# Short chained clears on GpSimd between the row scatters of a cross-attention and mixture-of-experts kernel

## The chip, the cores and the metric

The kernel runs on one core of one Trainium2 chip. The metric is the device time of one execution in microseconds (us). Three runs of the kernel before stand beside it; their median is 516.37 us. Engines are named as in the profile: PE is TensorE (matmuls) and PEld its weight loads, DVE is VectorE, ACT is ScalarE, POOL is GpSimd, SP is SyncE, which here only issues transfers.

## The reference

One layer over 4096 tokens (64 sequences of 64) of width 256: attention over a context and the tokens themselves, then a mixture of 32 experts, 4 for each token, beside a shared expert.

```python
h = layernorm(x)
q, k_new, v_new = h @ wq.T, h @ wk.T, h @ wv.T
k, v = concat([ctx, k_new]), concat([ctx, v_new])            # 64 + 64 keys of each sequence
x = x + softmax(q @ k.T / 16) @ v @ wo.T
h = layernorm(x)                                             # rows of 256
probs = softmax(h @ router.T)                                # 32 experts
topv, topi = top_k(probs, 4); topv = topv / sum(topv)
out = sum over the 4 experts e of topv[e] * (silu(h @ w_gate[e]) * (h @ w_up[e])) @ w_down[e]
out = out + sigmoid(h @ sgate_w) * ((silu(h @ sw_gate) * (h @ sw_up)) @ sw_down)
x = x + out
```

## The kernel before, in words

**Attention.** The tokens are worked in 16 blocks (`blocks`) of 256 tokens. Every engine runs its own software-pipelined loop over a step number n (L604 on ACT, L888 on PE, L1293 on DVE); what step n does for the different stages belongs to the blocks n+2 down to n-5. On PE a step has four groups of three-term products (L806: queries, keys, values, context values, 12 matmuls of 256 columns each), transposes, the scores (L981), the attended values (L998) and the router's logits (L1012).

**Routing and the scatter.** DVE normalizes the attended rows of block b into `rows[:, b % RING]` (`normalize`, L1222, in step b+3), a ring of RING = 6 buffers. It finds the 4 experts of each row, and the row's place with each, and as the last piece writes the weights into the ring (`weights`, L1289, in step b+5). GpSimd then scatters the block: 2 tiles of 128 rows times 4 experts are 8 indirect transfers (`send`, L481), each of 128 rows of 268 words, to the table `sent` in HBM. Before each transfer `send` waits for the block's numbers, names, weights and places; these come with L1289, so only a block's first transfer really waits. Before DVE writes block b+6 into the ring it waits for `rows_sent` of block b (L1317). After the last table entry is made, SP waits once for all scatters (L403 to L405) and then loads the experts' tiles (L417, L419), which PE turns (L1049).

**GpSimd's order** is written out in two loops (L496 to L502). For each step n there are 8 turns; turns 0 to 3 send what is left up to block n-6, turns 4 to 7 up to block n-5. So a step sends the second half of one block and then the first half of the next one. GpSimd takes nothing from the step number itself: it runs through this order and stops only at the semaphores in `send`. From step 17 on (n > blocks) each transfer is followed by one short clear (`breathe`, L490) of `pause`, four small tiles that nobody reads; the last 12 transfers are followed by three each. A clear there waits only for the one four places before it.

```python
for n in range(-2, blocks + 4):
    for turn in range(SENT_A_STEP):
        if may_send(n - 6 if turn < 4 else n - 5):
            send()
            if n > blocks:
                breathe(1)
```

**After attention**, PE works the shared expert for token groups 1 to 3, then 68 pairs of expert tiles, then the shared expert for groups 4 to 7, which end the kernel; GpSimd scatters the experts' results (L512).

Of the kernel before, what the change touches and what calls it, by code (L numbers as in the profile page):

```python
# [35 lines left out]
def build_xattn_moe(nc, x, ctx_t, wq_t, wk_t, wv, wo_t, router_t, w_gate_up, w_down,  # L36
# [34 lines left out]
    with ExitStack() as stack:  # L71
        def sb(name, shape, dt=F32):
            return stack.enter_context(nc.sbuf_tensor(name, shape, dt))
# [99 lines left out]
        pause = [sb(f"pause{n}", [P, 24]) for n in range(4)]  # L173
# [89 lines left out]
        def wait(eng, name, count):  # L263
            if count > 0:
                eng.wait_ge(S[name], count)
# [82 lines left out]
        def _(sp):  # L348
# [57 lines left out]
            for pair in range(pairs):  # L406
                u = pair % RING
                first, size = column_of(pair), QUARTER if mixed(pair) else P
                _, at = nc.values_load_multi_w_load_instructions(
                    tile_row[0:1, first:first + (5 if mixed(pair) else 2)], engines=[mybir.EngineType.SP],  # L410
                    min_val=0, max_val=EXPERTS * tokens - size,
                    skip_runtime_bounds_check_because="a tile's first row is a row of an expert's "
                                                      "region, at most its count less a tile on")
                wait(sp, "turned_psum", pair - RING + 1)
                wait(sp, "back_ready", (pair - RING) // 2 + 1)
                for q in range(P // size):
                    sp.dma_start(loaded[size * q:size * q + size, u, 0, :].bitcast(F32), sent[bass.ds(at[q], size), :]) \  # L417
                        .then_inc(tile_in[u], 16)
                sp.dma_start(loaded[:, u, 1, :].bitcast(F32), sent[bass.ds(at[P // size], P), :]).then_inc(tile_in[u], 16)  # L419
# [14 lines left out]
        @block.gpsimd  # L434
        def _(pool):
            c = S["consts"]
            pool.memset(ident[:, :], 0.0).then_inc(c, 1)
            pool.memset(before[:, :], 1.0).then_inc(c, 1)
            pool.memset(upto[:, :], 1.0).then_inc(c, 1)
            pool.memset(no_row, 0.0).then_inc(c, 1)  # L440
            pool.wait_ge(c, 4)
            pool.affine_select(out=ident[:, :], in_=ident[:, :], compare_op=ALU.not_equal, fill=1.0,
                               base=0, pattern=[[-1, P]], channel_multiplier=1).then_inc(c, 1)
            pool.affine_select(out=before[:, :], in_=before[:, :], compare_op=ALU.is_ge, fill=0.0,
                               base=-1, pattern=[[1, P]], channel_multiplier=-1).then_inc(c, 1)
            pool.affine_select(out=upto[:, :], in_=upto[:, :], compare_op=ALU.is_ge, fill=0.0,
                               base=0, pattern=[[1, EXPERTS]], channel_multiplier=-1).then_inc(c, 1)
            pool.iota(iota_e[:, :], [[1, EXPERTS]], base=0, channel_multiplier=0,
                      allow_small_or_imprecise_dtypes=True).then_inc(c, 1)
            pool.iota(place_no[:, :, :], [[P * TOP, tiles], [1, TOP]], base=P * slot_tiles, channel_multiplier=TOP,  # L450
                      allow_small_or_imprecise_dtypes=True).then_inc(c, 1)
            pool.iota(taken[0][:, 0, :], [[tokens // P, EXPERTS]], base=0, channel_multiplier=0,
                      allow_small_or_imprecise_dtypes=True).then_inc(c, 1)
            pool.memset(ones_h[:, :], 1.0).then_inc(c, 1)
            pool.iota(slot_no[:, :], [[P, slot_tiles]], base=0, channel_multiplier=1,
                      allow_small_or_imprecise_dtypes=True).then_inc(c, 1)
            pool.iota(region[:, :], [[0, 1]], base=0, channel_multiplier=tokens,
                      allow_small_or_imprecise_dtypes=True).then_inc(c, 1)
            pool.iota(lane[:, :], [[0, 1]], base=0, channel_multiplier=1,
                      allow_small_or_imprecise_dtypes=True).then_inc(c, 1)  # L460
            pool.iota(lanes_after[:, :], [[0, 1]], base=P - 1, channel_multiplier=-1,
                      allow_small_or_imprecise_dtypes=True).then_inc(c, 1)
            pool.memset(ones_e[:, :], 1.0).then_inc(c, 1)

            pool.wait_ge(c, POOL_CONSTS)

            sends = [(b, j, k) for b in range(blocks) for j in range(2) for k in range(TOP)]
            sent_now = [0]
            breaths = [0]

            def send():
                b, j, k = sends[sent_now[0]]
                sent_now[0] += 1
                u = b % RING
                if b == 0:
                    pool.wait_ge(S["no_rows"], 16 * HEADS)
                wait(pool, "numbered", b + 1)
                wait(pool, "named_ready", b + 1)
                wait(pool, "weights_ready", b + 1)
                wait(pool, "slot_ready", b + 1)  # L480
                pool.indirect_dma_start(  # L481
                    out=sent,
                    out_offset=bass.IndirectOffsetOnAxis(ap=slot[:, 2 * b + j, k:k + 1], axis=0),
                    in_=rows[:, u, j, :], in_offset=None).then_inc(rows_sent[u], 16)

            def breathe(times):

                for _ in range(times):
                    wait(pool, "breath", breaths[0] - len(pause) + 1)
                    pool.memset(pause[breaths[0] % len(pause)][:, :], 0.0).then_inc(S["breath"], 1)  # L490
                    breaths[0] += 1

            def may_send(n):
                return sent_now[0] < len(sends) and sends[sent_now[0]][0] <= n

# [3 lines that stand above are left out]
                        send()  # L499
                        if n > blocks:  # L500
                            breathe(1)
            while sent_now[0] < len(sends):  # L502
                send()
                breathe(3)

            for pair in range(pairs):
                u = pair % DOWNS
                wait(pool, "back_ready", pair // 2 + 1)
                wait(pool, "down_ready", pair + 1)
                for s in range(2):  # L510
                    t = 2 * pair + s
                    pool.indirect_dma_start(  # L512
                        out=returned,
                        out_offset=bass.IndirectOffsetOnAxis(ap=back[:, t:t + 1], axis=0),
                        in_=down_e[u][:, s, :], in_offset=None).then_inc(down_sent[u], 16)

        @block.scalar
        def _(act):
# [174 lines left out]
            def experts_to_copy(pair):  # L693

                first = column_of(pair)
                more = 7 if mixed(pair + 2) else 0
                _, values = nc.values_load_multi_w_load_instructions(
                    tile_expert[0:1, first:first + 4 + more], engines=[mybir.EngineType.Activation],
                    min_val=0, max_val=EXPERTS - 1,
                    skip_runtime_bounds_check_because="a tile's first row over the rows of a region "  # L700
                                                      "is the number of an expert")
                copied_e[pair], copied_e[pair + 2] = values[0:4], values[7:11]
# [85 lines left out]
        def _(pe):  # L788
# [288 lines left out]
            def experts_of(pair):  # L1077
                first = column_of(pair) + (4 if mixed(pair) else 0)
                _, values = nc.values_load_multi_w_load_instructions(
                    tile_expert[0:1, first:first + (1 if mixed(pair) else 2)], engines=[mybir.EngineType.PE],  # L1080
                    min_val=0, max_val=EXPERTS - 1,
                    skip_runtime_bounds_check_because="a tile's first row over the rows of a region "
                                                      "is the number of an expert")
                return values
# [678 lines left out]
```

## Time and profile before

| | |
|---|---|
| median of 3 runs | 516.37 us (515.13 to 516.96) |
| span of the profiled execution | 667.5 us |
| busy share of the span | PE 86%, PEld 72%, DVE 54%, ACT 43%, POOL 40% |
| mean granted TensorE clock | 0.903 of full speed |

For the profiled execution the page gives its span alone, no time around it. It is 151 us longer than the median of the runs, so its durations are those of a slower execution, and only its order and its ratios are taken over without care. The attention loop is the part from some 20 us to 250 us of the span, the rest of routing and the shared expert's first groups follow until 340 us, the experts' tiles until 593 us, and the last shared groups until the end.

### The profile page before, as it was taken

The numbers are of one execution on the slowest core, as the hardware profiler recorded it, in microseconds if no ns is written. First come the engines' busy times: TensorE is split into PE (matmuls) and PEld (weight loads), VectorE is DVE, ScalarE is ACT, GpSimd is POOL, SyncE is SP. The second block draws the span as 40 slices with busy tenths as digits, with TensorE's granted clock in tenths as the row PEclk, the third lists the DMA queues.
The fourth block names the chain that finished last, engine by engine and source line by source line (L and its number), as shares of the span: only waits on it lengthen the run. The fifth ranks groups of instructions, "written<-read, shape, count | busy, mean of one in ns | idle before, by whom it ended". The sixth has DMA issues, their size and how long they took to land. (4 is left out here: it accounts for less than half of the span.)

```text
span 667.5 us, 13365 instructions
## 1 busy us (share of the span) xinstructions
PE 574.4 (86%) x3945; PEld 478.3 (72%) x3945; DVE 363.5 (54%) x1199; ACT 288.7 (43%) x719; POOL 269.4 (40%) x344
## 2 busy tenths in 40 slices
PE   8998787788887777899998988778877898979998
PEld 7997777677777565677886666656666676658886
DVE  5575455555555351565553635445454444536998
ACT  5775444555444440613463545444454544401111
POOL 1004444445555458380034544445454454560000
PEclk9999788987778788699997977988989978989999
DMA  5573544444433322293145444544444544228996
GB/s 160 181 227 128 170 156 129 144 134 145 138 123 113 110 76 107 70 244 98 31 130 148 131 140 124 140 136 139 130 140 140 150 131 132 87 86 330 368 340 230
DMA packets 65956, 100.77 MB, mean 151 GB/s; under 512 B 9856, under 2 KB 52864, under 8 KB 65792
## 3 DMA queue, kind: packets, MB, share of 16 engines
q1 hardware_dynamic: 48704, 60.30, 30.6%
q0 software_dynamic: 12672, 35.41, 14.7%
q10 hardware_dynamic: 4512, 4.23, 1.9%
q8 instruction: 34, 0.56, 0.4%
q14 instruction: 34, 0.28, 0.1%
HBM read 55.92 MB, written 43.97 MB: 150 GB/s over the span
## 5 line engine op out<-in xcount | busy, mean ns | idle before, releaser
L512 POOL DMA_INDIRECT returned<-arena,back x136 | 130.6, 960 | 171.7 <-DVE back L1629 81.5
L481 POOL DMA_INDIRECT sent<-rows,slot x128 | 129.9, 1015 | 159.2 <-issue 82.7
L1100 PE MATMUL bank<-w_gu,arena 128*128 x416 | 94.7, 363 | 26.6 <-issue 16.6
L1100 PEld LDWEIGHTS bank<-w_gu,arena 128*128 128x128 f32 x416 | 73.0, 205 | 32.8 <-issue 32.8
L1580 DVE TENSOR_TENSOR arena<-bank,arena 128x192 f32<-128x192 f32 x68 | 24.2, 356 | 113.5 <-ACT arena L737 94.5
L737 ACT ACTIVATE arena<-bank 128x192 f32<-128x192 f32 x68 | 22.3, 329 | 127.0 <-remote 70.5
L806 PE MATMUL bank<-w_hi_all,att_split 128*128 128x256 f32 x256 | 56.8, 314 | 18.6 <-issue 18.6
L1597 DVE TENSOR_SCALAR arena<-bank,back_to 128x256 f32<-128x256 f32 x136 | 59.0, 476 | 6.3 <-remote 5.3
L806 PE MATMUL bank<-att_split,w_hi_all 128*128 128x256 f32 x256 | 55.5, 336 | 1.4 <-issue 1.3
L710 ACT COPY hnt<-w_gu 128x384 f32 x128 | 55.7, 509 | 0.0
L806 PEld LDWEIGHTS bank<-w_hi_all,att_split 128*128 128x128 f32 x256 | 42.4, 208 | 18.2 <-issue 18.2
L806 PE MATMUL bank<-hnt_rounded,ws_hi 128*128 128x512 f32 x160 | 51.0, 412 | 2.6 <-issue 2.6
L806 PEld LDWEIGHTS bank<-att_split,w_hi_all 128*128 128x128 f32 x256 | 47.7, 248 | 4.7 <-issue 4.6
L539 ACT ACTIVATE act_t<-bank 128x512 f32<-128x512 f32 x24 | 14.2, 598 | 82.9 <-PE bank L806 66.6
L1049 PE MATMUL bank<-ident_r,loaded 128*128 128x128 f32 x272 | 46.0, 295 | 0.4 <-issue 0.4
L850 PE MATMUL bank<-ws_d,act_t 128*128 128x256 f32 x192 | 43.3, 381 | 1.0 <-DVE act_t L1241 1.0
L731 ACT COPY arena<-bank 128x512 f32<-128x512 f32 x68 | 39.5, 582 | 8.9 <-PE bank L1049 2.5
L850 PEld LDWEIGHTS bank<-ws_d,act_t 128*128 128x128 f32 x192 | 36.1, 190 | 6.4 <-DVE act_t L1241 1.4
L806 PEld LDWEIGHTS bank<-hnt_rounded,ws_hi 128*128 128x128 f32 x160 | 31.6, 197 | 10.9 <-issue 4.0
L1049 PEld LDWEIGHTS bank<-ident_r,loaded 128*128 128x128 f32 x272 | 32.6, 148 | 9.0 <-issue 2.8
L806 PE MATMUL bank<-w_lo_all,att_split 128*128 128x256 f32 x128 | 30.3, 310 | 6.8 <-issue 6.5
L1311 DVE TENSOR_REDUCE negmax<-bank 128x2 f32<-128x256 f32 x16 | 6.7, 422 | 51.8 <-remote 51.8
(216 smaller groups left out, 1128.6 us busy)
## 6 DMA issues: line engine op xcount, KB each, us to landing
arena<-returned SPq DMA_DIRECT2D x16, 1024.0 KB, 7.2
loaded<-sent SPq DMA_DIRECT2D x104, 134.0 KB
w_gu<-w_gate_up SPq DMA_DIRECT2D x32, 192.0 KB
sent<-rows SPq DMA_DIRECT2D x4, 1072.0 KB, 6.2
loaded<-sent SPq DMA_DIRECT2D x128, 33.5 KB
resid<-x SPq DMA_DIRECT2D x16, 256.0 KB, 2.9
att_plain<-ctx_t SPq DMA_DIRECT2D x16, 256.0 KB, 3.1
out<-resid ACTq DMA_DIRECT2D x7, 512.0 KB, 4.9
```

The source lines that it names most:

```text
L481: pool.indirect_dma_start(out=sent, out_offset=bass.IndirectOffsetOnAxis(ap=slot[:, 2 * b + j, k:k + 1], axis=0), in_=rows[:, u, j, :], in ...
L512: pool.indirect_dma_start(out=returned, out_offset=bass.IndirectOffsetOnAxis(ap=back[:, t:t + 1], axis=0), in_=down_e[u][:, s, :], in_offs ...
L539: act.activation(act_t[:, f, :], gate_banks[f % 2][:, :], ACT.Silu) \
L710: last = act.copy(gu_copy[:, q, :, :], w_gu[:, :, bass.ds(copied_e[pair][q], 1), :] .rearrange("p c e f -> p c (e f)"))
L731: act.copy(gt[pair % 2].rearrange("p s c q -> p (s c q)"), gt_banks[pair % 2][:, :]) \
L737: act.activation(act_e[pair % 2], gu_views[pair % 2][:, :, 0:F], ACT.Silu) \
L806: last = pe.matmul(out_view, stationary(s_part, c), moving(m_part, c), start=(n == 0 and c == 0), stop=(n == 2 and c == DC - 1))
L850: last = pe.matmul(sum_banks[t // 2][:, 256 * (t % 2):256 * (t % 2) + 256], act_t[:, f, P * t:P * t + P], ws_d[:, f, :], start=(f == 0 and ...
L1049: last = pe.transpose(gt_banks[pair % 2][:, at:at + P].bitcast(F32R), loaded[:, u, s, P * c:P * c + P], ident_r[:, :])
L1100: last = pe.matmul(view[:, s, :], rows_t[:, s, c, :], w_gu[:, c, bass.ds(e[s - 2 + len(e)], 1), :] .rearrange("p e f -> p (e f)"), start=( ...
L1580: dve.tensor_tensor(act_e[pair % 2], gu_views[pair % 2][:, :, F:2 * F], act_e[pair % 2], ALU.mult).then_inc(S["act_e_ready"], 1)
L1597: last = dve.tensor_scalar(down_e[u][:, s, :], down_banks[pair % 2][:, D * s:D * s + D], back_to[:, pair // 2 % 4, 2 * (pair % 2) + s, 0:1 ...
```

## The change

Within attention (steps up to n = 16), behind turn 2, turn 5 and turn 7 of each step that sends, GpSimd makes four short clears of `pause`. Each of them waits for the one just before it. The semaphore `breath` has no other reader than GpSimd.

```diff
+            def rest(times):
+
+                for _ in range(times):
+                    wait(pool, "breath", breaths[0])
+                    pool.memset(pause[breaths[0] % len(pause)][:, :], 0.0).then_inc(S["breath"], 1)
+                    breaths[0] += 1
+
             def may_send(n):
                 return sent_now[0] < len(sends) and sends[sent_now[0]][0] <= n
 
@@ -499,6 +506,8 @@
                         send()
                         if n > blocks:
                             breathe(1)
+                        elif turn in (2, 5, 7):
+                            rest(4)
```

## Rows read from the trace of the kernel before

**Rows 1.** The page, parts 1 and 2: engines, slices, and the clock granted to PE.

```profile
PE 574.4 (86%) x3945; PEld 478.3 (72%) x3945; DVE 363.5 (54%) x1199; ACT 288.7 (43%) x719; POOL 269.4 (40%) x344
...
PEclk9999788987778788699997977988989978989999
```

**Rows 2.** Waits from 56 to 236 us: engine and line, waited for, us, times, longest.

```profile
POOL sent L481 <- DVE rows L1289: 60.8, 11, 6.2
DVE negmax L1311 <- remote: 51.8, 11, 9.6
ACT logits L616 <- remote: 50.2, 11, 6.6
```

**Rows 3.** Timeline of POOL over one block's eight transfers and the next's first.

```profile
118.94 0.96 POOL L481 DMA_INDIRECT sent<-rows,slot  x1 [5.77 <-DVE rows L1289]
120.20 1.12 POOL L481 DMA_INDIRECT sent<-rows,slot  x1 [0.30 <-issue]
121.63 1.35 POOL L481 DMA_INDIRECT sent<-rows,slot  x1 [0.30 <-issue]
123.28 0.96 POOL L481 DMA_INDIRECT sent<-rows,slot  x1 [0.30 <-issue]
...
128.33 0.96 POOL L481 DMA_INDIRECT sent<-rows,slot  x1 [0.30 <-issue]
134.49 0.95 POOL L481 DMA_INDIRECT sent<-rows,slot  x1 [5.21 <-DVE rows L1289]
```

**Rows 4.** Timeline of POOL: clears unchained and a chain of waits at the start.

```profile
1.15 0.31 POOL L440 MEMSET rows<- 128x268 f32 x1
1.70 0.29 POOL L442 TENSOR_SCALAR_AFFINE_SELECT ident<-ident 128x128 f32<-128x128 f32 x1 [0.24 <-POOL rows L440]
...
249.30 0.97 POOL L481 DMA_INDIRECT sent<-rows,slot  x1 [0.17 <-issue]
250.27 0.14 POOL L490 MEMSET pause<- 128x24 f32 x1
250.57 0.97 POOL L481 DMA_INDIRECT sent<-rows,slot  x1 [0.16 <-issue]
...
282.43 0.23 POOL L490 MEMSET pause<- 128x24 f32 x3
```

**Rows 5.** Line L1222 on DVE, 56 to 236 us: ns min/median/max.

```profile
L1222 DVE TENSOR_SCALAR rows<-resid,both_moments,rstd x24: 403/406/429, 65.4 to 235.7; 128x256 f32<-128x256 f32 x24
L1222 DVE TENSOR_SCALAR att_plain<-resid,both_moments,rstd x20: 396/404/415, 55.8 to 198.1; 128x256 f32<-128x256 f32 x20
```

**Rows 6.** The same line in the drain, 249 to 251 us.

```profile
L1222 DVE TENSOR_SCALAR rows<-resid,both_moments,rstd x2: 404/469/534, 249.5 to 249.8; 128x256 f32<-128x256 f32 x2
```

**Rows 7.** Timeline of DVE in the step of rows 3.

```profile
118.65 0.72 DVE L1222 TENSOR_SCALAR att_plain<-resid,both_moments,rstd 128x256 f32<-128x256 f32 x2
...
122.06 0.69 DVE L1296 TENSOR_TENSOR att_split<-att_plain,att_split 128x512 fp32r<-128x512 f32 x1
124.03 0.69 DVE L1300 TENSOR_TENSOR att_split<-bank,att_split 128x512 fp32r<-128x512 f32 x1 [1.28 <-issue]
127.88 0.42 DVE L1311 TENSOR_REDUCE negmax<-bank 128x2 f32<-128x256 f32 x1 [3.16 <-remote]
128.22 0.75 DVE L1222 TENSOR_SCALAR rows<-resid,both_moments,rstd 128x256 f32<-128x256 f32 x2
```

**Rows 8.** Timeline of POOL: first and last transfer of block 1.

```profile
71.70 0.96 POOL L481 DMA_INDIRECT sent<-rows,slot  x1 [5.28 <-DVE rows L1289]
...
81.13 0.96 POOL L481 DMA_INDIRECT sent<-rows,slot  x1 [0.30 <-issue]
```

**Rows 9.** SP's wait for all scatters, its first tile load, and PE's first use.

```profile
SPq L405 <- DMA sent<-rows,slot: 21.8, 1, 21.8
...
303.79 0.38 SPq L417 DMA_DIRECT2D loaded<-sent  x1
...
L1049 PE MATMUL bank<-ident_r,loaded x272: 223/249/668, 324.3 to 576.1; 128*128 128x128 f32 x136
```

**Rows 10.** Timeline of PE: four products at either level of its clock.

```profile
119.10 0.64 PE L806 MATMUL bank<-w_hi_all,att_split 128*128 128x256 f32 x4
...
131.92 1.05 PE L806 MATMUL bank<-att_split,w_hi_all 128*128 128x256 f32 x4
```

**Rows 11.** Stretches between blocks' first transfers: POOL busy, granted clock, DMA share, GB/s.

```profile
118.94:134.49 15.55, 8.21 (x9) 0.89 0.48 148
134.49:150.09 15.60, 8.24 (x8) 0.80 0.42 135
150.09:166.23 16.14, 8.24 (x9) 0.77 0.45 141
```

## The prediction

> **What bounds the kernel now.** I began with the engines' busy shares and the clock row of the page [rows 1]: PE is busy for 86% of the span and POOL for 40%. PE is the engine to watch, and its granted clock falls below full speed in most slices of attention. Then the waits inside attention, from 56 to 236 us [rows 2]. POOL waits 60.8 us in 11 places for the weights of L1289, about 5.5 us in each step; DVE waits 51.8 us in 11 places before its row maximum L1311 and ACT 50.2 us before the logits copy, both behind PE's work. No wait of PE, ACT or DVE in that view is put down to POOL or to a transfer. The step is thus paced by PE with DVE and ACT behind it, and POOL is the engine with room. The stretches between the first transfers of successive blocks show the pace: 15.55, 15.60 and 16.14 us a step, of which POOL is busy 8.2 [rows 11].
>
> The reader should then look at one block's transfers [rows 3]. Eight transfers run from 118.94 to 129.29 us, 0.96 us each and 0.30 us apart, and POOL is idle for 5.21 us before the next block's first at 134.49. The second and third take 1.12 and 1.35 us, the ones that lie beside DVE's burst of SBUF work.
>
> **The change, part by part.** How many clears. Sending begins with step 5, whose turns 4 to 7 send, so two rests fall there; steps 6 to 16 have three each. That is 2 + 33 = 35 rests of four clears, 140 in all. Counted in a block's own order, a rest comes behind its second, fourth and seventh transfer, since a step's turns 4 to 7 are a block's first half. Nothing is removed and no instruction of another engine is touched. The first clear of attention's rests and the breaths later on use the same semaphore, and later breaths find their counts long reached.
>
> One rest. A clear takes 0.14 us [rows 4]. Clears that don't chain follow each other closely: three take 0.23 us together. A chained one has to see its predecessor's semaphore; the nearest row is the first of the constants, which starts 0.24 us after the clear it waits for has ended (1.46 to 1.70 us, rows 4). So a chained clear costs 0.38 us, a rest 0.14 + 3 x 0.38 = 1.28 us. The next transfer then starts 0.17 us behind the last clear instead of 0.30 us behind the last transfer, so a rest holds the queue up by 1.28 + 0.17 - 0.30 = 1.15 us. From below, were the chain free (three in 0.23 us, four in about 0.31), a rest would add 0.18 us. I take 1.15 us, because the row with a real wait is nearer to what is added.
>
> One block. Three rests are 3.5 us. The eight transfers then last from 118.94 to about 132.7 us, and less if the third transfer, moved from 121.63 to about 122.8, no longer lies beside DVE's burst and gives back its 0.39 us. The next block's weights come in time for a start at 134.49 us. About 2 us of the idle 5.21 us are left, and they hide the whole of the change on POOL. Cost on the path: 0.
>
> Who waits for the later transfers. First, DVE before it refills a ring buffer. At 128.22 us it writes block 7 (rows 7, second L1222), which needs block 1's transfers; the last of these started at 81.13 us [rows 8]. That is 46 us of room against 3.5 us of delay. Second, SP before the experts' tiles. Its wait for the scatters lasts 21.8 us and its first load goes out at 303.79 us, but PE first turns a tile at 324.3 us [rows 9], 20 us later. Besides, that wait is for the last blocks, whose transfers are outside the part that gets rests, and POOL stands idle ahead of them. Cost: 0 for both.
>
> Side effects on DVE. Twenty-four and twenty L1222 instructions in attention take 403 to 429 and 396 to 415 ns, whether a transfer runs beside them or not [rows 5]. So transfers don't slow DVE. A clear can: the one L1222 pair in the drain that has a clear beside it (250.27 us, rows 4) has one instruction of 534 ns [rows 6], 128 ns over the usual 406 and about a clear's own length. The Trainium skill says in "SBUF — State Buffer", section "Who interferes with whom", that a VectorE instruction in a two-port mode and a GpSimd instruction exclude each other and that the later one waits in full; by this rule, the trace agrees for the clear with its 128 ns, while rows 5 show nothing of the sort for the transfers. Where do the clears fall? With the times above, at 121.3 to 122.6, 125.0 to 126.3 and 129.9 to 131.2 us of the step shown. DVE's L1222 pairs lie at 118.65 to 119.37 and 128.22 to 128.97 us, outside all three, and the second and third rest lie mostly in its idle time [rows 7]. I count 0 collisions, with 4 a step as the upper bound.
>
> Sum: 0 + 0 + 0. The profiled execution would stay at a span of 667.5 us. The page gives no time around the span, and the median of the runs, 516.37 us, is 151 us below it; since my sum is zero it carries over unscaled, and the forecast is 516.4 us. The measurement can tell about 0.3%, or 1.55 us, from nothing.
>
> **Rivals.**
>
> 1. DVE is held up by the clears (slower). This is the one cost the trace has shown. Place: the four L1222 of each of 12 steps. Price: 48 x 0.128 = 6.1 us if every one met a clear and all lay on the path, giving 522.5 us. It decides from 12 collisions on the path (12 x 0.128 = 1.54 us). For it: the timed runs are faster than the profiled one, so DVE's instructions stand closer around the rests there; the third rest is only 0.9 us behind a pair. Against it: DVE waits 4.7 us a step before L1311, which swallows 0.128 us easily. A likely size is one or two hits a step, 1.5 to 3 us: 518 to 519.5 us. Chance 0.11.
>
> 2. POOL becomes the pace in the timed runs. Scaled by 516.4/667.5, a step of 15.6 us is 12.1 us, while POOL's block, if it does not scale, takes 13.8 us and 0.9 us for the release: 2.6 us too much. Over 11 blocks the transfers fall 28 us behind. The ring's room scales to 36 us, so DVE still doesn't stop; the idle 5 and 10 us ahead of the last blocks take up 12 us of it, and the last 16 us meet the 20 us (scaled 16) between SP's first load and PE's first turn. The result lies at the edge of a cost: 516.4 up to some 520 us. Against it, POOL's own gaps probably shrink too. Chance of over 1.55 us: 0.07.
>
> 3. PE gains its clock or another engine gains from thinner traffic (faster). Four products take 0.64 us at the full 2.4 GHz and 1.05 us at 1.2 GHz [rows 10], 0.10 us each; a step has 48 of them, so one whole step at the higher level is worth 4.9 us: 511.5 us. Neighbouring steps already differ, 0.89, 0.80 and 0.77 of full speed, with the same work [rows 11], so small shifts in what PE waits for can move it, and the transfers would be spread over 13.8 instead of 10.3 us of a step in which the transfer engines are busy for 0.42 to 0.48. Against it: I find no row by which a later transfer makes DVE, ACT or PE earlier, and step lengths don't follow the granted clock (15.60 at 0.80, 16.14 at 0.77, 15.55 at 0.89). The same path could lose time as well, but nothing leads into it. Half a step to a step is 2 to 5 us: 511.5 to 514.5 us. Chance 0.30, rather high for want of a row, since the profiled execution is so unlike the timed ones that a cause could hide between them.
>
> That the change does nothing at all (clears that end inside the 0.30 us gap) would look like my forecast.
>
> **How the numbers follow.** No effect on the path has 0.52 and gives 516.4 us, with a range of its own of 514.9 to 517.9 us. Faster by over 0.3% has 0.30, slower has 0.11 + 0.07 = 0.18. The range for 8 in 10 takes in the same case, rival 3 down to a full step regained and rivals 1 and 2 up to about half of rival 1's bound: 511.5 to 519.5 us, leaving out some 0.08 on either side.
>
> **What the changed profile would show.** 140 more clears at a new line on POOL, four to a group, some 0.38 us apart; the idle time before each block's first transfer down from 5.2 to about 2 us with the waiter and releaser unchanged; the last transfer still ending near 299 us; L1222 at 396 to 429 ns; waits of DVE at L1311 unchanged; steps of 15.5 to 16.1 us. I am wrong if that idle time is gone, if many L1222 take over 0.5 us, or if the steps' lengths or the clock granted in them change together by more than the spread among the three shown.

## The result: slower by 7.7%, and the profile after

The changed kernel takes 553.88 us (median of 4 runs, 553.51 to 555.38) beside 515.75 us for the kernel before, a ratio of 1.077 (95% interval 1.071 to 1.083). Here and below a ratio is the record's own estimate with its interval, not the quotient of the two medians printed beside it; the two differ by up to 1.4%. The forecast was no change, 516.4 us, in a range of 511.5 to 519.5. It is 38 us off, on the side to which it gave 0.18.

One thing has to be said first, as nothing else can be read without it. The chips on which these runs were made fall into two groups. On one, the kernel before takes 512 to 519 us; on the other, 641 to 681 us. Of the four chips of the experiments, numbers 2, 4 and 8 are slow in this sense and number 15 is fast. The times that came with the kernel are of the first group, and the profile on which the prediction rests (span 667.5 us) shows the pace of the second. The profile after (span 553.0 us) is again of the first.

The page of the changed kernel, parts 1 and 2:

```profile
PE 511.7 (93%) x3945; PEld 433.7 (78%) x3945; DVE 363.1 (66%) x1199; ACT 287.0 (52%) x719; POOL 286.6 (52%) x484
...
PE   7999999999978799991399999999999999999998
...
PEclk9999999999979999997599999999999999999999
```

Against [rows 1] PE's clock is hardly ever held back, and PE is busy for 93% of a shorter span. What stands out is a hole in PE's row in slices 19 and 20; the timelines below put it at 251 to 270.5 us. The waits of the same kernel over its whole span (engine and line, waited for, us in total, times, longest), the second list those of SP:

```profile
POOL sent L481 <- issue: 96.6, 118, 52.3
...
DVE rows L1231 <- DMA sent<-rows,slot: 25.4, 5, 6.1
PE bank L1058 <- DMA loaded<-sent: 23.8, 11, 19.6
...
POOL sent L481 <- DVE rows L1298: 2.7, 4, 1.0
```

```profile
SPq L405 <- DMA sent<-rows,slot: 57.8, 1, 57.8
```

The line for POOL's wait for the weights has shrunk from 60.8 us in 11 places [rows 2] to 2.7 us in 4: GpSimd hardly ever runs dry, it has a backlog. Two kinds of waits are new against the old profile, DVE's for the ring (L1231, L1222 of the kernel before) and PE's for a loaded tile (L1058, L1049 of before), the longest 19.6 us. SP's wait for all scatters is 57.8 us long instead of 21.8 [rows 9]. The timelines of DVE and of POOL show the two paces:

```profile
108.42 0.41 DVE L1320 TENSOR_REDUCE negmax<-bank 128x2 f32<-128x256 f32 x1
...
118.03 0.41 DVE L1320 TENSOR_REDUCE negmax<-bank 128x2 f32<-128x256 f32 x1
```

```profile
101.75 0.96 POOL L481 DMA_INDIRECT sent<-rows,slot  x1 [0.30 <-issue]
102.71 0.66 POOL L497 MEMSET pause<- 128x24 f32 x4
104.36 0.97 POOL L481 DMA_INDIRECT sent<-rows,slot  x1 [1.00 <-issue]
...
107.97 0.66 POOL L497 MEMSET pause<- 128x24 f32 x4
109.33 0.98 POOL L481 DMA_INDIRECT sent<-rows,slot  x1 [0.70 <-issue]
```

An attention step takes 9.61 us, not 15.6. GpSimd needs 13.4 to 14.4 us for a block, 13.9 in the mean (the first block's first transfer starts at 56.0 us, the twelfth's at 208.9). It falls some 4 us behind in every step. The end of that queue is what PE finally waits for; SP's, POOL's and PE's timelines at that place:

```profile
263.91 0.97 POOL L481 DMA_INDIRECT sent<-rows,slot  x1 [0.16 <-issue]
```

```profile
267.47 0.38 SPq L417 DMA_DIRECT2D loaded<-sent  x1
```

```profile
245.56 5.34 PE L859 MATMUL bank<-ws_d,act_t 128*128 128x256 f32 x24
270.50 0.72 PE L1058 MATMUL bank<-ident_r,loaded 128*128 128x128 f32 x4 [19.60 <-DMA loaded<-sent]
```

### The profile page after: what moved, and what is told of

It reads as the page before. It is cut to its first block and busy times, and to the rows that moved or that the text cites. A ratio compares the mean times of both kernels' runs of the same rounds, so it can differ in the third digit from the quotient of the medians.

```text
span 553.0 us, 13505 instructions
## 1 busy us (share of the span) xinstructions
PE 511.7 (93%) x3945; PEld 433.7 (78%) x3945; DVE 363.1 (66%) x1199; ACT 287.0 (52%) x719; POOL 286.6 (52%) x484
## 5 line engine op out<-in xcount | busy, mean ns | idle before, releaser
L481 POOL DMA_INDIRECT sent<-rows,slot x128 | 128.7, 1005 | 102.3 <-issue 96.6
L1109 PE MATMUL bank<-w_gu,arena 128*128 x416 | 83.8, 339 | 0.0
L1109 PEld LDWEIGHTS bank<-w_gu,arena 128*128 128x128 f32 x416 | 66.4, 191 | 0.3
L1058 PE MATMUL bank<-ident_r,loaded 128*128 128x128 f32 x272 | 41.9, 278 | 24.2 <-DMA loaded<-sent 23.8
L1058 PEld LDWEIGHTS bank<-ident_r,loaded 128*128 128x128 f32 x272 | 30.0, 142 | 36.3 <-issue 20.3
L548 ACT ACTIVATE act_t<-bank 128x512 f32<-128x512 f32 x24 | 14.4, 599 | 75.9 <-PE bank L815 75.9
L815 PE MATMUL bank<-w_hi_all,att_split 128*128 128x256 f32 x256 | 49.0, 294 | 0.0
L815 PE MATMUL bank<-att_split,w_hi_all 128*128 128x256 f32 x256 | 44.0, 284 | 0.0
L815 PEld LDWEIGHTS bank<-w_hi_all,att_split 128*128 128x128 f32 x256 | 37.4, 192 | 0.9 <-issue 0.9
L815 PEld LDWEIGHTS bank<-att_split,w_hi_all 128*128 128x128 f32 x256 | 36.7, 193 | 0.1
L1278 DVE SCALAR_TENSOR_TENSOR resid<-bank,shared_gate,resid 128x256 f32<-128x256 f32 x28 | 11.7, 478 | 30.8 <-PE bank L859 30.4
L1231 DVE TENSOR_SCALAR rows<-resid,both_moments,rstd 128x256 f32<-128x256 f32 x32 | 12.1, 418 | 25.4 <-DMA sent<-rows,slot 25.4
```

The lines of the kernel that those rows point to most:

```text
L481: pool.indirect_dma_start(out=sent, out_offset=bass.IndirectOffsetOnAxis(ap=slot[:, 2 * b + j, k:k + 1], axis=0), in_=rows[:, u, j, :], in ...
L548: act.activation(act_t[:, f, :], gate_banks[f % 2][:, :], ACT.Silu) \
L815: last = pe.matmul(out_view, stationary(s_part, c), moving(m_part, c), start=(n == 0 and c == 0), stop=(n == 2 and c == DC - 1))
L1058: last = pe.transpose(gt_banks[pair % 2][:, at:at + P].bitcast(F32R), loaded[:, u, s, P * c:P * c + P], ident_r[:, :])
L1109: last = pe.matmul(view[:, s, :], rows_t[:, s, c, :], w_gu[:, c, bass.ds(e[s - 2 + len(e)], 1), :] .rearrange("p e f -> p (e f)"), start=( ...
```

## The experiments

Theories, as the expectations name them. **A**: where PE is at full rate, GpSimd's queue sets when the experts' tiles can be loaded, and a rest costs what it delays the queue. **B**: the clears hold DVE up. **C**: the clears cost by themselves. **D**: at the slower pace, rests keep PE at full rate. **E**: the pace of PE is a matter of the chip alone.

### The kernel before once more (e0_before)

No edit.

> The kernel before once more, for a profile at the pace of the timed runs; the profile on which the prediction rested was 151 us longer than they are. Theory A (GpSimd is the pace): an attention step is about 9.6 us, as in the profile of the changed kernel, a block's eight transfers take 8 x 1.27 = 10.2 us, GpSimd has no idle time before a block's first transfer from the first blocks on, the last transfer starts near 225 us (263.9 us with the change), and PE turns its first tile some 7 us later, near 232 us. Theory B (DVE is held up by the clears): GpSimd has idle time in each step, as in the old profile, and the attention loop itself ends tens of us earlier than with the change.

Measured: 669.0 us beside 671.8 (ratio 0.997). This chip was of the slow group, so the run showed the old profile's picture once more (last transfer at 295 us) and told nothing of theory A; it told that the old picture is no accident of one execution.

### All clears ahead of the first transfer (e2_front, e2b_front)

```diff
+            rest(140)
             for n in range(-2, blocks + 4):
...
-                        elif turn in (2, 5, 7):
-                            rest(4)
```

> All 140 chained clears stand ahead of the first transfer, where GpSimd has 52 us of idle time, and none between transfers. Theory A: the clears cost nothing there, 516 us, ratio to before 1.00, within 0.005. Theory C (the clears cost by themselves, by their semaphore traffic or as code): 554 us, ratio 1.07. Theory B doesn't tell: 516 us too.

> All 140 chained clears ahead of the first transfer, once more. On the first chip of the experiments (672 us for the kernel before) this left the time as it was (ratio 1.001). Where the kernel before takes 516 us, theory A says 516 us, ratio 1.00 within 0.005: the clears cost nothing where GpSimd has nothing to send. If the clears as such cost there, 554 us.

Measured: ratio 1.001 (0.996 to 1.007) on the slow chip, and 515.6 us beside 517.0, ratio 0.999 (0.995 to 1.002), on a fast one. Theory C is out: the same clears cost nothing where GpSimd waits anyway. The second run also stands in for a profile of the kernel before at full rate, since its transfers are the same. Its page, and its timelines of DVE, POOL, SP and PE:

```profile
PE 502.3 (98%) x3945; PEld 428.3 (83%) x3945; DVE 364.2 (71%) x1199; ACT 287.1 (56%) x719; POOL 289.5 (56%) x484
...
PEclk9999999999999999999999999999999999999999
```

```profile
106.68 0.41 DVE L1319 TENSOR_REDUCE negmax<-bank 128x2 f32<-128x256 f32 x1
...
116.29 0.41 DVE L1319 TENSOR_REDUCE negmax<-bank 128x2 f32<-128x256 f32 x1
```

```profile
107.80 0.96 POOL L481 DMA_INDIRECT sent<-rows,slot  x1 [0.30 <-issue]
...
118.67 0.96 POOL L481 DMA_INDIRECT sent<-rows,slot  x1 [0.30 <-issue]
...
225.28 0.97 POOL L481 DMA_INDIRECT sent<-rows,slot  x1 [0.16 <-issue]
```

```profile
228.84 0.38 SPq L417 DMA_DIRECT2D loaded<-sent  x1
```

```profile
234.73 0.98 PE L1057 MATMUL bank<-ident_r,loaded 128*128 128x128 f32 x8
```

Steps of 9.61 us again, and transfers 0.30 us apart from block to block: counting blocks from 0, block 5's first starts at 107.8 us and block 6's at 118.7, so eight of them take 10.9 us, already more than a step. GpSimd has no room at all in this kernel. PE reaches its first tile turn at 234.7 us without waiting, 9.4 us after the last transfer starts. With the change, where PE does wait, it is 6.6 us after. So about 3 us of room lie between the end of the queue and PE, and no more.

These rows show one more thing, which the prediction had the other way round. DVE's L1230 (L1222 of the kernel before) usually takes 0.41 us. Here 9 of its 45 instructions in attention take 523 to 622 ns, with no clear anywhere near. Each starts 0.43 to 0.53 us before the end of a transfer's issue on GpSimd and ends 0.09 us behind it. The lines are the view of L1230 from 50 to 170 us, then DVE's timeline (two instructions together, 571 ns the first) and POOL's:

```profile
L1230 DVE TENSOR_SCALAR rows<-resid,both_moments,rstd x25: 394/408/622, 49.7 to 165.4; 128x256 f32<-128x256 f32 x25
```

```profile
107.01 0.89 DVE L1230 TENSOR_SCALAR rows<-resid,both_moments,rstd 128x256 f32<-128x256 f32 x2
```

```profile
106.53 0.96 POOL L481 DMA_INDIRECT sent<-rows,slot  x1 [0.30 <-issue]
```

PE is busy without a break through this part, so these hits cost nothing here.

### Clears not chained (e1_unchained, e1b_unchained)

```diff
-                    wait(pool, "breath", breaths[0])
+                    wait(pool, "breath", breaths[0] - len(pause) + 1)
```

> The same 140 clears at the same places, but each waits for the clear four before it instead of for the one just before. Theory A: what counts is how much later the next transfer starts; three unchained clears and the gap behind them take 0.40 us, four then some 0.5 us in place of 0.30 us, 0.2 us for each of 35 rests, so +7 us: 523 us, ratio 1.014. Theory B (a clear blocks DVE for its own length): as many clears at the same places, so nearly all of the loss stays, 545 to 554 us.

> The 140 clears unchained. Where the kernel before takes 516 us, theory A: 0.2 us for each of 35 rests, less the 3 us by which PE's first tile turn is later than it need be there, 520 us, ratio 1.004 to 1.014. If the number of clears counts, 554 us. Where it takes 640 to 680 us: no gain, as before (ratio 1.0065 there).

Both runs fell on slow chips: ratio 1.0065 (1.002 to 1.011) on the first; 657.1 us beside 657.7 on the other, without an interval. The question for the fast group was not answered. For the slow group they say that these 140 clears gain nothing when they aren't chained; a group of four then makes the gap between two transfers 0.45 us instead of 0.30.

### Rests of eight (e3_double, e3b_double)

```diff
-                            rest(4)
+                            rest(8)
```

> Rests of eight chained clears instead of four. Theory A: GpSimd is already the pace, so every us added to its queue shows in full in the time. By the spacing of the changed kernel (four chained clears end 0.66 to 0.95 us after the transfer) four more take 0.7 to 1.1 us, times 35 is 25 to 39 us on top of 554: 579 to 593 us, and the kernel's time grows by just as much as the start of the last transfer does. Theory B: at most 48 SBUF instructions of DVE can be hit, 0.13 us each, so the time stays within 6 us of 554.

> Rests of eight chained clears. Where the kernel before takes 516 us, theory A: on the other chips eight clears put the last transfer at 288 us against 265 us for four, so the time is 22 to 26 us over that of the changed kernel, 576 to 582 us, ratio 1.12. Where it takes 640 to 680 us: about 644 us as before (ratio 0.96).

Measured, on slow chips both times: 644.0 us beside 671.8, ratio 0.962 (0.954 to 0.969), and 635.9 beside 657.7, 0.978 (0.960 to 0.997). This was the surprise that theory D was made for: on these chips rests of eight make the kernel faster than it is without rests.

### The changed kernel on a chip of the slow group (a1_after)

No edit.

> The changed kernel once more, beside the kernel before on the same chip. The kernel before has now been seen at two paces: 516 us, and 672 us on the chip of the first four experiments, where PE's products in attention come 213 ns apart in most steps instead of 120. Theory A+D (GpSimd's queue sets the end of attention where PE is at full rate; where PE would be at half rate, the rests keep it at full rate in attention, as eight clears did): 554 us where the kernel before takes 516; where the kernel before takes 672, the last transfer starts near 264 us as in the first profile after, and with the 340 us that follow PE's first tile turn on that chip this gives 605 to 625 us. Theory E (only the rate of PE differs between chips, and the rests have nothing to do with it): at the slow pace GpSimd has 5 us of idle time a step, the rests fit in, 665 to 675 us.

Measured: 612.4 us (608.4 to 617.8) beside 653.3, ratio 0.937 (0.923 to 0.952). Theory D's 605 to 625 us holds, theory E's 665 to 675 does not. The very change that costs 7.7% on the fast group gains some 6% here: all four executions (608.4 to 617.8 us) lie below all nineteen of the kernel before (641.5 to 667.3). The windows of this run from 54 to 175 us, and those of e6_no_breaths on the same chip, whose attention is that of the kernel before, show where; the columns are the stretch, us busy and instructions of PE, PEld, DVE, ACT and POOL, granted clock, share of the transfer engines, GB/s:

```profile
54.00:115.00 61.00, 60.55 (x579) 56.86 (x577) 52.00 (x214) 44.91 (x127) 42.64 (x87) 1.00 0.59 189
115.00:175.00 60.00, 54.49 (x456) 47.73 (x455) 40.83 (x165) 38.35 (x108) 40.90 (x88) 0.94 0.49 156
```

```profile
54.00:115.00 61.00, 50.79 (x374) 44.88 (x374) 31.30 (x132) 27.68 (x80) 33.01 (x32) 0.83 0.46 145
115.00:175.00 60.00, 49.93 (x384) 42.12 (x383) 35.56 (x143) 29.64 (x86) 32.97 (x32) 0.94 0.48 152
```

Without rests PE not only runs at a lower clock, it also stands idle for 10 us in each of the two stretches. The place where the kernels part can be seen in PE's timeline. Up to 60.7 us both run alike. Then the kernel before (first fence, e0_before) stops for 0.7 to 0.8 us after every few products, beside eight scatters in a row on GpSimd (54.43 to 64.63 us). Those gaps are put down to "issue": PE waits for nothing that the profile shows. Between them its products are still 120 ns apart, and the granted clock is still 1.00; only then does it go to 0.50, from 65.1 to 71.9 us (second fence, windows), and the products to 213 ns, which are the 2.4 and the 1.2 GHz level. With the rests (third fence, a1_after) neither happens:

```profile
61.78 0.40 PE L806 MATMUL bank<-w_hi_all,att_split 128*128 128x256 f32 x2 [0.72 <-issue]
...
63.23 0.49 PE L806 MATMUL bank<-w_hi_all,att_split 128*128 128x256 f32 x2 [0.83 <-issue]
...
67.56 1.05 PE L806 MATMUL bank<-att_split,w_hi_all 128*128 128x256 f32 x4
```

```profile
60.50:65.10 4.60, 2.19 (x14) 1.87 (x13) 1.14 (x4) 0.60 (x2) 3.21 (x4) 1.00 0.37 107
65.10:71.90 6.80, 6.15 (x28) 5.79 (x28) 5.20 (x25) 4.08 (x13) 1.67 (x2) 0.50 0.66 212
```

```profile
65.01 0.64 PE L815 MATMUL bank<-w_hi_all,att_split 128*128 128x256 f32 x4
```

### One rest a step, and rests in the first steps only (e4_one_rest, e9_first_steps, e9b_first_steps)

```diff
-                        elif turn in (2, 5, 7):
+                        elif turn == 7:
```

```diff
-                        elif turn in (2, 5, 7):
+                        elif turn in (2, 5, 7) and n <= 8:
```

> One rest a step (behind turn 7) instead of three: 12 rests, 48 clears. Theory A, where the kernel before takes 516 us: 12 x 1.1 us = 13 us, 529 us. Where it takes 672 us: theory D expects part of the gain of three rests if the spread of the transfers decides, 610 to 660 us; theory E expects 672 us.

> Rests of four only in steps 5 to 8: 11 rests, blocks 0 to 3. Where the kernel before takes 516 us, theory A: 11 x 1.15 = 12.6 us, 528 us. Where it takes 640 to 680 us: if PE, once at full rate with a backlog on GpSimd, stays there, the best of both, 590 to 605 us; if each step needs its own rests, PE falls to half rate soon after block 3 (near 100 us) and 630 to 655 us.

> Rests of four only in steps 5 to 8 (11 rests). Where the kernel before takes 516 us it took 525 us (ratio 1.014), and should again. Where it takes 640 to 680 us: if a step at full rate keeps the next one there, as GpSimd then has a backlog and no burst follows a release, full rate in all of attention and the last transfer near 237 us, some 30 us earlier than with all rests: 580 to 600 us. If each step needs its own rests, products 213 ns apart from about 105 to 120 us on, and 630 to 655 us.

e4 (slow chip): ratio 1.002 (0.996 to 1.008); 12 rests gain nothing that can be measured. e9 (fast chip): 525.0 us beside 517.0, ratio 1.014 (1.008 to 1.019): 8.0 us for 11 rests, where 12.6 were expected; the 3 us of room account for most of the difference. DVE waits for no scatter in that run, so the ring isn't needed for the loss. e9b (slow chip): 646.9 beside 657.7, ratio 0.990 (0.983 to 0.997), a gain of 1% at most. By the distances of the row maxima its steps last 9.3 to 11.7 us from the first transfer up to 100 us. The rests end with block 3 at 106 us; then comes one step of 31.4 us, in which PE stops again and again, for up to 4.4 us, with nothing shown that it waits for, and from 131 us on steps of 14.0 to 16.7 us. So full rate does not last by itself: the rests are needed all along.

### The rests late, and no clears at all (e5_late, e6_no_breaths)

```diff
-                        elif turn in (2, 5, 7):
+                        elif n >= 12 and turn != 3:
```

The first edit is against the changed kernel, the second against the kernel before.

```diff
                         send()
-                        if n > blocks:
-                            breathe(1)
...
                 send()
-                breathe(3)
```

> The same 35 rests, all behind transfers of steps 12 to 16 (blocks 6 to 11), so that the ring of six buffers stops DVE little or not at all. Theory A, where the kernel before takes 516 us: the last transfer is as late as with the change, 554 us, with much less than 25 us of waits of DVE for scatters; if instead those waits of DVE were the cost, 516 to 530 us. Where the kernel before takes 672 us: theory D says PE falls to half rate as soon as the first transfers go out without rests, near 60 us, so nothing or little is gained, 665 to 680 us.

> The kernel before without any clear between transfers, also none in the last part: 24 single ones, which add 0.01 us each by the rows, and 12 times three, which add 0.10 us each. Theory A, where the kernel before takes 516 us: if GpSimd's queue is the pace there too, 1.2 us are gained, 514.5 us; if PE is the pace, 515.8 us. Where it takes 672 us: theory D says denser transfers can only hurt, 672 us or up to 10 us more; theory E says 672 us.

Both on a slow chip. e5: 638.3 beside 653.3, ratio 0.980 (0.968 to 0.992), more than theory D gave it. Its row maxima show both paces in one run, first without rests, then with them (the first rest starts at 151.8 us):

```profile
62.31 0.42 DVE L1320 TENSOR_REDUCE negmax<-bank 128x2 f32<-128x256 f32 x1 [2.37 <-remote]
79.13 0.42 DVE L1320 TENSOR_REDUCE negmax<-bank 128x2 f32<-128x256 f32 x1 [2.38 <-remote]
...
151.10 0.42 DVE L1320 TENSOR_REDUCE negmax<-bank 128x2 f32<-128x256 f32 x1 [1.49 <-remote]
160.61 0.41 DVE L1320 TENSOR_REDUCE negmax<-bank 128x2 f32<-128x256 f32 x1
```

The four steps from 151 us on last 8.1 to 9.5 us; the last four of e6 on the same chip, without rests, 13.7 to 16.5 us. PE went back to full rate when rests came in, so the expectation that a lost rate is lost for good was wrong. e6: ratio 1.004 (0.999 to 1.010); the clears of the last part do nothing that can be measured on a slow chip.

### A pause without a clear (e7_landed)

Against the kernel before:

```diff
+            def landed():
+
+                b, j, k = sends[sent_now[0] - 1]
+                pool.wait_ge(rows_sent[b % RING], 16 * (BLOCK_SCATTERS * (b // RING) + TOP * j + k + 1))
+
...
                             breathe(1)
+                        elif turn in (2, 5, 7):
+                            landed()
```

> No clears at all in attention: at the same 35 places GpSimd waits instead until the transfer it has just issued has landed. Theory D1 (what keeps PE at full rate is that the transfers are thinned): where the kernel before takes 640 to 680 us, attention's products stay 120 ns apart as with the rests, and the time is near that of the changed kernel plus or minus 35 times the difference of the pauses; 600 to 640 us. Theory D2 (the clears themselves do it): products at 213 ns from about 62 us on, 640 to 680 us. Where the kernel before takes 516 us, theory A says that the time grows by the pauses alone, 554 us if a landing takes as long as a rest, more if longer.

On a fast chip: 594.6 us beside 517.0, ratio 1.150 (1.144 to 1.156). The gap between two transfers is 1.7 to 4.4 us long in attention, where a rest makes it 1.4 to 1.8:

```profile
96.11 1.03 POOL L481 DMA_INDIRECT sent<-rows,slot  x1 [2.38 <-DMA sent<-rows,slot]
...
101.70 0.95 POOL L481 DMA_INDIRECT sent<-rows,slot  x1 [3.30 <-DMA sent<-rows,slot]
```

With 35 such waits and no clear the kernel loses 78 us, about 2.2 us each: the loss goes with the length of the pause, and no clear is needed for it, so theory B has nothing left to explain. Whether an idle pause keeps PE at full rate on a slow chip was not tried.

### Rests of two (e8_rest2, e8b_rest2)

```diff
-                            rest(4)
+                            rest(2)
```

> Rests of two chained clears instead of four. Theory A: the pause is part clears (0.66 us for four) and part the later start of the next transfer (0.70 to 1.00 us instead of 0.17), so two clears still cost 0.7 to 0.9 us each: where the kernel before takes 516 us, 540 to 547 us. Where it takes 640 to 680 us: full rate kept in attention and 30 to 45 us gained if a pause of this length is enough.

> Rests of two chained clears in all steps. Where the kernel before takes 516 us it took 541 us (ratio 1.047), and should again. Where it takes 640 to 680 us: a shorter pause of some 0.6 us; if it is enough for full rate in attention, the last transfer comes near 249 us and the time is 595 to 610 us, below that of the changed kernel; if not, products 213 ns apart from 62 us on and 640 to 680 us, as with unchained clears.

e8 (fast): 540.7 us beside 517.0, ratio 1.047 (1.044 to 1.050). e8b (slow): 627.3 beside 657.7, ratio 0.968 (0.957 to 0.979). By both ratios two clears lie between none and four, though the slow ratios are of different chips. Rests of eight, unchained clears and a single rest a step were never run on a fast chip.

### Taken together

Fast group. The traces start up to 1.7 us apart (read off the first row maximum); that is taken out here, and everything is against e2b_front.

| kernel | pauses | last transfer later by | first tile turn later by | time over the kernel before |
|---|---|---|---|---|
| first steps only | 11 x 4 | 10.5 us | 7.4 us | 8.0 us |
| rests of two | 35 x 2 | 23.2 us | 20.1 us | 23.7 us |
| the change | 35 x 4 | 36.9 us | 34.0 us | 38.1 us |
| waits for a landing | 35 | 77.3 us | 74.3 us | 77.6 us |

The last column is of medians, the others of one execution each; that of the first row took 529.0 us, 4 us over its median. Each us by which the queue ends later, less 3 us, is a us of PE's first tile turn. What follows the turn takes 282.5 us with the change and 278.5 without (ends of the spans less the turns), the missing 4 us. Some 3 us of them are PE's clock, which went to 0.50 within the hole and stayed there over the first 6.1 us of tiles (windows of the changed kernel); PE is busy for 273.7 us behind the turn instead of 270.7. The other us is PE's further waits for tiles, 4.2 us instead of 3.1.

```profile
256.10:270.50 14.40, 0.00 (x0) 0.03 (x1) 0.00 (x0) 0.00 (x0) 8.02 (x28) 0.50 0.30 95
270.50:276.60 6.10, 5.51 (x19) 4.61 (x20) 0.40 (x1) 1.17 (x2) 0.00 (x0) 0.50 0.48 121
```

Slow group, by chip, as these chips differ among themselves. "Attention" is the time from the first row maximum to the last; e2b_front on the fast chip stands below for comparison.

| chip | run | rests | attention | first tile turn at | span |
|---|---|---|---|---|---|
| 4 | e0_before | none | 208.8 us | 330.0 us | 666.7 us |
| 4 | e1_unchained | 35 x 4, not chained | 214.0 us | 333.9 us | 671.0 us |
| 4 | e3_double | 35 x 8 | 159.4 us | 304.6 us | 644.0 us |
| 2 | e6_no_breaths | none | 197.3 us | 314.9 us | 649.7 us |
| 2 | e4_one_rest | 12 x 4 | 195.2 us | 304.1 us | 637.0 us |
| 2 | e5_late | 35 x 4, late | 171.4 us | 297.7 us | 633.8 us |
| 2 | a1_after | 35 x 4 | 145.4 us | 279.2 us | 615.4 us |
| 8 | e1b_unchained | 35 x 4, not chained | 196.7 us | 321.3 us | 657.0 us |
| 8 | e9b_first_steps | 11 x 4 | 194.2 us | 306.2 us | 640.5 us |
| 8 | e8b_rest2 | 35 x 2 | 159.9 us | 290.1 us | 623.5 us |
| 8 | e3b_double | 35 x 8 | 160.8 us | 299.2 us | 635.7 us |
| 15 | e2b_front | none | 139.2 us | 234.7 us | 513.2 us |

What follows the first tile turn takes 333 to 340 us on every slow chip, with rests or without, so the gain is an earlier turn. (e4's profiled execution was the shortest of its ten, 639.2 us beside a median of 647.3, so its row flatters it.) With the change attention takes as long on a slow chip (145.4 us) as on a fast one (145.0 us). One rest a step, or rests at the start only, leave it nearly as it was. Rests of eight hold it up in another way: DVE then waits 46.3 us for the ring, with four clears 23.7 us.

## Why the prediction was wrong, step by step

**What bounds the kernel.** The prediction let the step be paced by PE and gave GpSimd 5 us of room in it. That is the reading of [rows 2, 3], and it is right for the execution shown. It fails for the timed runs: there the step is 9.61 us, and a block's transfers take 10.9 us. This is the step that failed, and with it the sentence "About 2 us of the idle 5.21 us are left, and they hide the whole of the change on POOL".

**One rest.** Taken at 1.15 us, between 0.18 and 1.15. Measured: the gap between two transfers is 1.46 us in the mean instead of 0.30, so 1.16 us each. The size was right, its make-up wasn't: four chained clears mostly last 0.66 us, not 1.28, but the next transfer then starts 0.51 to 1.00 us behind them, mostly 0.70, not 0.17. That the last transfer is 36.9 us later, 1.05 us for each rest and not 1.16, fits what the prediction expected of one transfer: once shifted, it no longer lies beside DVE's work and gets shorter. The issue of all 128 takes 128.7 us instead of 132.3.

**One block.** The shift of 3.5 us a block was nearly right: a block takes 13.9 us, and 13.8 was worked out. Multiplied out, the prediction's own price gives 40 us for 35 rests, and the loss is 38. That these two are so close is partly luck, as 3 us of room and 4 us behind the turn nearly cancel.

**Who waits.** Both waiters were named with their places. The ring's 46 us of room held in the old profile; at full rate the backlog grows until DVE waits 25.4 us in 5 places, yet this lies beside PE's later wait. The other, SP's wait before the tiles, was given 20 us of room, and "POOL stands idle ahead of them": at full rate there is no idle time and 3 us of room. That is where the loss comes out.

**DVE held up by the clears** (rival 1). Not the cause. e2b shows the clears without cost elsewhere, and e7 the loss without clears. "So transfers don't slow DVE. A clear can" was a wrong reading of [rows 6]: the instruction of 534 ns runs from 249.82 to 250.36 us, and so ends 0.09 us behind a transfer's issue (249.30 to 250.27), as the nine of e2b_front do with no clear near; the clear starts only at 250.27, 0.45 us after the instruction that it was said to hold up, so the trace doesn't agree for the clear as the prediction says. The longest of the changed kernel (585 ns from 70.31 us) ends 0.09 us behind a transfer's issue too (70.81 us). In [rows 5] none is long because at that pace no instruction happened to lie there.

**POOL becomes the pace** (rival 2). This is what happened, and it had a chance of 0.07. It scaled the step by the ratio of the two times, 15.6 to 12.1 us. But the slow execution is not slower by one factor all through: what follows the first tile turn takes 343.2 us in it and 278.5 at the fast pace (1.23 times), the attention loop 209.2 and 139.2 us (1.50 times). The evidence was in the trace. Before 51 us, ahead of the first transfer, the row maxima of the kernel before follow each other in 7.5 to 9.7 us (timeline of DVE, kernel before):

```profile
32.60 0.41 DVE L1311 TENSOR_REDUCE negmax<-bank 128x2 f32<-128x256 f32 x1
41.34 0.41 DVE L1311 TENSOR_REDUCE negmax<-bank 128x2 f32<-128x256 f32 x1
50.99 0.41 DVE L1311 TENSOR_REDUCE negmax<-bank 128x2 f32<-128x256 f32 x1
65.09 0.42 DVE L1311 TENSOR_REDUCE negmax<-bank 128x2 f32<-128x256 f32 x1 [3.08 <-remote]
```

The waits of PE from 56 to 236 us, and the window from the first row maximum to the last, in the kernel before (first two fences) and in e2b_front (third), say what the 70 us are:

```profile
PE bank L806 <- issue: 29.3, 51, 1.2
```

```profile
16.83:226.00 209.17, 174.22 (x1358) 157.45 (x1357) 112.68 (x443) 108.04 (x292) 89.77 (x88) 0.86 0.47 150
```

```profile
14.87:154.10 139.23, 139.23 (x1332) 130.69 (x1332) 113.72 (x443) 105.85 (x291) 87.30 (x154) 1.00 0.67 207
```

Half of them, 35 us, is PE standing idle (209.2 less 174.2), most of it in 51 gaps with nothing shown that it waits for; the other half is PE busy for longer with the same work, at a clock of 0.86. The prediction weighed the clock alone, in rival 3, and passed over the 51 gaps, which stood in the view from which [rows 2] were taken. An engine that stops without a cause in the profile doesn't pace a step by its work. From the old profile alone it can be estimated: from 56 to 236 us, 11.5 steps, 29.3 us of gaps are 2.5 us a step, and a granted clock of 0.83 is 2.7 us of 15.6. A step without both is 10.4 us, below the 13.8 worked out for a block with rests, and the backlog over eleven blocks nearly 40 us, less the room at its end.

**PE gains its clock** (rival 3, 0.30). Wrong for the fast group, where the granted clock is 1.00 without the change (0.999 to 1.000 in thirteen runs on chip 15) and there is nothing to gain. On the slow chips it is just what the change does, and by more than the half step to a step that it was given: 41 us of 653 by the medians, idle gaps and clock together. "I find no row by which a later transfer makes DVE, ACT or PE earlier" was a fair reading, and no reason against it.

**What would show it wrong.** The test named first, the idle time before each block's first transfer gone, is the one that came true.

## What to carry to other kernels

When the profiled execution is much longer than the timed runs, find out where the difference lies before any slack is read from it: compare the same loop's steps early and late and the spacing of equal matmuls, look for gaps of the pacing engine that nothing in the profile explains, and work the sum once more with the shorter step. An in-order queue that has no slack at the fast pace hands every added pause to whatever waits for its last entry, here about 1.05 us for each of 35 rests. And a change can be a gain on one chip and a loss on the next: say for which of them it is made.

## What the runs showed of the hardware

Two groups of chips ran one and the same kernel in about 516 us and in about 640 to 680 us. On the faster, PE's products in attention keep to 120 ns; on the slower they alternate between 120 and 213 ns, with a granted clock of 0.84 from 54 to 175 us in e0_before, and the experts' part is longer too (244 us from the first tile turn to the last in e0_before, 193 us in e2b_front).

On the slower chips the order on GpSimd alone moves PE's idle time and its clock. The instructions of the other engines are the same, and PE has the same products in front of it. With rests, which make the gap between two transfers 1.4 to 1.8 us behind two, two and three transfers, PE has no unexplained gap before a product and holds the 2.4 GHz level through attention up to 155 us; with a gap of 0.45 us at the same places it does neither. In the trace the idle gaps come first, at a granted clock of 1.00, and the lower clock after them. The mean density of the transfers can't be what decides, since it is higher with the rests (8 in 13.9 us) than without (8 in 15.5 us). Whether it is the unbroken run of transfers that stops PE, or something that goes with it, no run here separates, and why only some chips show it stays open.

On the fast chip PE's clock fell too where PE stood still: to 0.50 from 256.1 to 276.6 us, within and behind the hole of the changed kernel. It cost some 3 us of PE's time behind the turn.

A chain of four short clears on GpSimd mostly takes 0.66 us, about 0.17 us a clear, but a scatter behind it starts only 0.51 to 1.00 us after its end, where one behind three unchained clears starts after 0.16 us. About half of the pause is this late start.

A scatter's issue on GpSimd can hold up a `tensor_scalar` on DVE (L1230 in e2b_front): an instruction that started 0.33 to 0.53 us before the end of the issue didn't end until 0.09 us behind it, and took up to 0.62 us instead of 0.41. The 534 ns of [rows 6] fit the same pattern.
